# Weighting whole in each step, sums inverted by way of memory, and another opening in a 16-head attention

## What is computed

```python
x = x + layernorm(attention1(layernorm(x)))      # x: 2 x 2048 x 256, float32
x = x + layernorm(ffn_stack(layernorm(x)))       # two layers of windowed attention and gated feed forward

def attention1(x):                               # 16 heads of 16, 2 batches: 32 heads
    q, k, v = rope(x @ Wq.T + bq), rope(x @ Wk.T + bk), x @ Wv.T + bv
    scores = einsum('bhtd,bhsd->bhts', q, k) / 4 # 2048 x 2048 for each of 32 heads
    attn = softmax(scores, axis=-1)
    return einsum('bhts,bhsd->bhtd', attn, v) @ Wo.T + bo
```

## Time and profile before

| | |
|---|---|
| median of 3 runs | 3482.14 us (3476.58 to 3494.06) |
| the profiled execution | 3474.07 us, of which the trace spans 3472.3 us |
| PE, DVE, ACT, POOL busy | 93%, 72%, 65%, 23% of the span |
| projections, until the attention block | 0 to 124 us |
| opening of the attention | 140 to 203 us |
| steps of the attention | 203 to 1866 us |
| end of the attention, output phase | 1866 to 1945 us |
| feed forward and final phase | 1945 to 3472 us |
| DMA | 107.50 MB, mean 31 GB/s |

### The profile page before, as it was taken

The page is one execution under the profiler, slowest core; times in us unless marked ns, Lnnn a source line. Parts: engine busy times, 40 slices in busy tenths (PEclk is TensorE's granted clock), DMA queues, the critical chain, the costliest instruction groups (busy, mean ns, idle before and its releaser), DMA issues. The chain is left out here.

```text
span 3472.3 us, 61794 instructions
## 1 busy us (share of the span) xinstructions
PE 3231.1 (93%) x23464; PEld 2003.4 (58%) x23464; DVE 2487.7 (72%) x4740; ACT 2263.8 (65%) x4950; POOL 804.2 (23%) x992
## 2 busy tenths in 40 slices
PE   8799999999999999999996599999999999999996
PEld 7544333334433343434433478888888888888885
DVE  7458767778867787878862577777777777777775
ACT  5357657567765677757774566666666766676663
POOL 6400000000000000000001643344433444443442
PEclk9659868789977898969988799999999999999998
DMA  5413313133223233223222200000000000000001
GB/s 162 125 19 44 44 23 44 23 44 44 39 27 41 26 44 44 38 28 41 31 29 75 102 1 1 0 0 0 0 0 1 33 1 0 0 0 0 0 1 66
DMA packets 55354, 107.50 MB, mean 31 GB/s; under 512 B 21744, under 2 KB 34032, under 8 KB 48368
## 3 DMA queue, kind: packets, MB, share of 16 engines
q1 hardware_dynamic: 50608, 103.36, 16.8%
q10 hardware_dynamic: 4544, 1.38, 0.2%
HBM read 70.61 MB, written 25.17 MB: 28 GB/s over the span
## 5 line engine op out<-in xcount | busy, mean ns | idle before, releaser
L670 ACT ACTIVATE probs<-scores 128x512 f32<-128x512 f32 x2048 | 1114.9, 596 | 525.3 <-PE scores L607 489.6
L702 DVE TENSOR_REDUCE mx<-aux 128x1 f32<-128x1024 f32 x976 | 1190.6, 1224 | 364.6 <-PE aux L565 360.4
L565 PE MATMUL aux<-k_stack,q_stack 48*128 48x512 f32 x2000 | 943.1, 524 | 36.7 <-DVE mx L702 34.5
L607 PE MATMUL scores<-q_stack,k_stack 50*128 50x512 f32 x2048 | 857.9, 499 | 0.0
L619 PE MATMUL pv<-probs,v_ones 128*32 128x256 f32 x8192 | 745.5, 440 | 0.1
L607 PEld LDWEIGHTS scores<-q_stack,k_stack 50*128 50x128 f32 x2048 | 348.4, 209 | 507.4 <-ACT probs L670 469.1
L565 PEld LDWEIGHTS aux<-k_stack,q_stack 48*128 48x128 f32 x2000 | 396.0, 211 | 174.2 <-DVE mx L702 165.8
L619 PEld LDWEIGHTS pv<-probs,v_ones 128*32 128x32 f32 x8192 | 170.4, 114 | 342.0 <-issue 321.5
L536 POOL CAST m_parts<-head_max 128x16 fp32r<-128x16 f32 x32 | 6.3, 196 | 1516.6 <-DVE head_max L695 1516.6
L1242 PE MATMUL bank<-VO,w_sb 128*128 128x128 f32 x2816 | 328.8, 277 | 1.5 <-ACT VO L1329 1.5
L1242 PEld LDWEIGHTS bank<-VO,w_sb 128*128 128x128 f32 x2816 | 323.2, 194 | 2.5 <-ACT VO L1329 2.5
(11 more groups left out here) (175 smaller groups left out, 4664.0 us busy)
## 6 DMA issues: line engine op xcount, KB each, us to landing
q_stack<-qk_dram SPq DMA_DIRECT2D x192, 128.0 KB, 5.3
k_stack<-qk_dram SPq DMA_DIRECT2D x192, 128.0 KB, 7.5
qk_dram<-qkT_hi SPq DMA_DIRECT2D x32, 256.0 KB, 3.1
qk_dram<-qkT_lo SPq DMA_DIRECT2D x32, 256.0 KB, 3.6
VO<-o_stage SPq DMA_DIRECT2D x128, 32.0 KB, 8.3
totals<-o_stage SPq DMA_DIRECT2D x128, 32.0 KB, 7.9
out<-x_sb SPq DMA_DIRECT2D x9, 384.0 KB, 4.3
wqkv_sb<-in_wqkv SPq DMA_DIRECT2D x2, 1536.0 KB, 7.1
```

The costliest lines, as they stand in the source:

```text
L565: return nc.tensor.matmul(out, q_stack[max_rows, n % BODY, tile * P:(tile + 1) * P], k_stack[max_rows, n % BODY, keys * 512:(keys + 1) * 512],
L607: last = nc.tensor.matmul(out, k_stack[0:SCORE_ROWS, n % BODY, s * P:(s + 1) * P], q_stack[0:SCORE_ROWS, n % BODY, j * 512:(j + 1) * 512], ...
L670: nc.scalar.activation(probs[:, e % PROBS], scores[:, item_of_exp(e) % BANKS1], ACT.Exp, scale=float(D1) ** -0.5).then_inc(act_emptied, 1)
L702: nc.vector.tensor_reduce(mx[:, n % BODY, tile, half:half + 1], aux[:, unit % 2].rearrange("p a k -> p (a k)"), AX.X, ALU.max).then_inc(dv ...
```

## The change

- The weighting of a step is whole: four matmuls of 512 columns, two steps later, between block 1 and block 2. The two maximum tiles before it fill one unit of `aux`, the two after it the other. `pv` is copied one exponential later.
- The sums of a head go as one row for each block to `sums_dram`, come back as 128 partitions x 16, are inverted on DVE in one small instruction a head (`invert_sums`), go back to memory and are read from there 16 times over into `inverse`. For the last 8 heads DVE does half of the multiplications.
- In the opening the differences use rows 0 to 47 of PE and so the loads for scores; each maximum tile is issued between the two matmuls of a difference, and behind the second stands a matmul from row 64 on into `pv`, whose result nobody reads. Head 1 is loaded for scores before the opening, and POOL fills the minus ones buffer by buffer.
- Wo and its bias are loaded during the attention, into a buffer that the feed forward phase later uses for small tiles; these become views of it, with the same instructions.

```diff
         @block.sync
...
                 sp.wait_ge(pv_copied, n + 1)
-                if n % CHUNK == 0 and c > 0:
-                    sp.wait_ge(divided, BLOCKS * c)
                 for j in range(BLOCKS):
-                    for to, row in ((outputs[place:place + D1, c], VW * j), (totals[place:place + D1], VW * j + D1)):
-                        sp.dma_start(to[:, j * 512:(j + 1) * 512], o_stage[row:row + D1, n % 2]).then_inc(outputs_moved, 16)
+                    columns = slice(j * 512, (j + 1) * 512)
+                    sp.dma_start(sums_dram[0, n:n + 1, columns], o_stage[VW * j + D1:VW * j + D1 + 1, n % 2]).then_inc(sums_stored, 16)
+                    sp.dma_start(outputs[place:place + D1, c, columns], o_stage[VW * j:VW * j + D1, n % 2]).then_inc(outputs_moved, 16)
+
+            def load_sums(n):
+
+                sp.wait_ge(sums_stored, 16 * BLOCKS * (n + 1))
+                sp.dma_start(sums[:, n % 2], sums_dram[0, n].rearrange("(p c) -> p c", p=P)).then_inc(sums_loaded, 16)
+
+            def store_inverse(n):
+
+                sp.wait_ge(sums_inverted, n + 1)
+                sp.dma_start(sums_dram[1, n].rearrange("(p c) -> p c", p=P), sums[:, n % 2]).then_inc(inverse_stored, 16)
+
+            def spread_inverse(n):
+
+                sp.wait_ge(inverse_stored, 16 * (n + 1))
+                if n % CHUNK == 0 and n > 0:
+                    sp.wait_ge(divided, BLOCKS * (n // CHUNK))
+                sp.dma_start(inverse[n % CHUNK * D1:(n % CHUNK + 1) * D1], sums_dram[1, n].partition_broadcast(D1)).then_inc(inverse_loaded, 16)
 
             load(0, SECOND, for_max_loaded)
-            load(1, SECOND, for_max_loaded)
-            sp.wait_ge(minus_ones_made, 1)
-            load(0, 0, for_scores_loaded)
+            for n in range(2):
+                sp.wait_ge(minus_ones_made, n + 1)
+                load(n, 0, for_scores_loaded)
+                if n == 0:
+                    load(1, SECOND, for_max_loaded)
             load_rows(0)
+            load_output_weights(sp)
...
+                if n >= 2:
+                    store_inverse(n - 2)
                 if n >= 1:
                     move_outputs(n - 1)
                 if n + 1 < NH:
                     load_rows(n + 1)
+                if n >= 2:
+                    spread_inverse(n - 2)
+                if n >= 1:
+                    load_sums(n - 1)
+            store_inverse(NH - 2)
             move_outputs(NH - 1)
+            spread_inverse(NH - 2)
+            load_sums(NH - 1)
+            store_inverse(NH - 1)
+            spread_inverse(NH - 1)
...
         @block.gpsimd
...
-                pool.wait_ge(for_max_loaded[n], 16 * LOADS)
+                rows = slice(0, SPLIT_ROWS)
+                pool.wait_ge(for_scores_loaded[n], 16 * LOADS)
...
-                if n % CHUNK == 1 and n > 1:
-                    divide(n // CHUNK - 1)
+                if n % CHUNK == 2 and n > 2:
+                    for j in range(BLOCKS):
+                        divide(n // CHUNK - 1, j)
+                    pool.wait_ge(divided, BLOCKS * (n // CHUNK))
...
         @block.tensor
...
+            def weigh(step):
+
+                n, s = divmod(step, TB)
+                if s == 0:
                     pe.wait_ge(v_made, n + 1)
                     if n:
                         pe.wait_ge(pv_copied, n)
-                pe.wait_ge(act_emptied, item_of_exp(BLOCKS * (TB * n + s + 1) - 1) + 1)
-                columns = slice(half * HALF, (half + 1) * HALF)
+                pe.wait_ge(act_emptied, item_of_exp(BLOCKS * (step + 1) - 1) + 1)
                 for j in range(BLOCKS):
...
+                    last = nc.tensor.matmul(pv[VW * j:VW * (j + 1)], v_ones[:, n % BODY, s, :], probs[:, (BLOCKS * step + j) % PROBS],
+                                            start=(s == 0), stop=(s == TB - 1), skip_group_check=True, tile_position=(0, VW * j))
+                last.then_inc(pv_done, 1)
+
+            def first_difference(t, k):
...
+                out, rows = for_act(2 * t + k), slice(0, SPLIT_ROWS)
+                nc.tensor.matmul(out, q_stack[rows, n, tile * P:(tile + 1) * P], k_stack[rows, n, (2 + k) * 512:(3 + k) * 512], start=True, stop=False)
+                for_dve(t, k)
+                nc.tensor.matmul(out, q_minus_first[rows, t], k_stack[rows, n, k * 512:(k + 1) * 512], start=False, stop=True).then_inc(act_filled, 1)
+                nc.tensor.matmul(pv[:], q_stack[max_rows, n, tile * P:(tile + 1) * P], k_stack[max_rows, n, k * 512:(k + 1) * 512], start=True, stop=True)
...
                     if rows_here(p, i):
                         maximum_rows(p // 2 + 1)
-                    if j == 0:
-                        weigh_earlier(step, 2, 1)
-                    if j == (3 if step % TB == 1 else 2):
-                        weigh_earlier(step, 1, 0)
...
+                    if j == 1 and step >= 2:
+                        weigh(step - 2)
+            weigh(NH * TB - 2)
+            weigh(NH * TB - 1)
 
         @block.scalar
...
-                    if i == BLOCKS + 1 and p % 2 == 0 and p > 0:
+                    if i == BLOCKS + 2 and p % 2 == 0 and p > 0:
                         copy_outputs(p // 2 - 1)
...
         @block.vector
...
-            def invert_totals(c, j):
-
-                dve.wait_ge(outputs_moved, 16 * 2 * BLOCKS * CHUNK * (c + 1))
-                here = totals[:, j * 512:(j + 1) * 512]
-                nc.vector.reciprocal(here, here).then_inc(inverted, 1)
+            def invert_sums(n):
+
+                dve.wait_ge(sums_loaded, 16 * (n + 1))
+                nc.vector.reciprocal(sums[:, n % 2], sums[:, n % 2]).then_inc(sums_inverted, 1)
...
-                    if p % 2 == 1 and i % SPAN == SPAN - 1 and n % CHUNK == 0 and n > 0:
-                        invert_totals(n // CHUNK - 1, i // SPAN)
-            for j in range(BLOCKS):
-                invert_totals(NH // CHUNK - 1, j)
...
+                    if p % 2 == 0 and i == 3 and n >= 2:
+                        invert_sums(n - 2)
+            invert_sums(NH - 2)
+            invert_sums(NH - 1)
+            for j in range(BLOCKS // 2, BLOCKS):
+                divide(NH // CHUNK - 1, j)
```

More of the change, by code:

```diff
@@ L365 @@
 VW = 32
-HALF = 256
 SPAN = TB // 2
@@ L566, in score_for_max @@
                                         start=True, stop=True)
-            def difference(t, k, out):
-                n, tile = divmod(t, TB)
-                piece = [i for i, (head, start, stop) in enumerate(Q_MINUS_PIECES) if head == n and start <= tile < stop][0]
-                pe.wait_ge(q_minus_made, piece + 1)
-                minus = q_minus_first[max_rows, t]
-                pe.wait_ge(for_max_loaded[n % BODY], 16 * LOADS * (n // BODY + 1))
-                nc.tensor.matmul(out, q_stack[max_rows, n % BODY, tile * P:(tile + 1) * P], k_stack[max_rows, n % BODY, (2 + k) * 512:(3 + k) * 512], start=True, stop=False)
-                nc.tensor.matmul(out, minus, k_stack[max_rows, n % BODY, k * 512:(k + 1) * 512], start=False, stop=True).then_inc(act_filled, 1)
             def for_act(item):
@@ L615, in weigh @@
                         pe.wait_ge(pv_copied, n)
-                pe.wait_ge(act_emptied, item_of_exp(BLOCKS * (TB * n + s + 1) - 1) + 1)
-                columns = slice(half * HALF, (half + 1) * HALF)
+                pe.wait_ge(act_emptied, item_of_exp(BLOCKS * (step + 1) - 1) + 1)
                 for j in range(BLOCKS):
-                    last = nc.tensor.matmul(pv[VW * j:VW * (j + 1), columns], v_ones[:, n % BODY, s, :], probs[:, (BLOCKS * (TB * n + s) + j) % PROBS, columns],
-                                            start=(s == 0 and half == 0), stop=(s == TB - 1 and half == 1), skip_group_check=True, tile_position=(0, VW * j))
-                if half == 1:
-                    last.then_inc(pv_done, 1)
-            def weigh_earlier(step, back, half):
-                if step >= back and step - back < NH * TB:
-                    weigh((step - back) // TB, (step - back) % TB, half)
+                    last = nc.tensor.matmul(pv[VW * j:VW * (j + 1)], v_ones[:, n % BODY, s, :], probs[:, (BLOCKS * step + j) % PROBS],
+                                            start=(s == 0), stop=(s == TB - 1), skip_group_check=True, tile_position=(0, VW * j))
+                last.then_inc(pv_done, 1)
+            def first_difference(t, k):
+                n, tile = divmod(t, TB)
+                piece = [i for i, (head, start, stop) in enumerate(Q_MINUS_PIECES) if head == n and start <= tile < stop][0]
+                pe.wait_ge(q_minus_made, piece + 1)
+                pe.wait_ge(for_scores_loaded[n], 16 * LOADS)
+                out, rows = for_act(2 * t + k), slice(0, SPLIT_ROWS)
[3 more added lines that the diff above has]
+                nc.tensor.matmul(pv[:], q_stack[max_rows, n, tile * P:(tile + 1) * P], k_stack[max_rows, n, k * 512:(k + 1) * 512], start=True, stop=True)
             for t in range(OPENING):
@@ L632, in _ @@
                 for k in range(2):
```

(8 more changed lines are left out.)

83 lines of the change are left out of this document (43 added, 40 removed).

## The result

| | before | after |
|---|---|---|
| median | 3484.73 us of 4 runs (3476.58 to 3494.06) | 3163.7 us of 4 runs (3163.28 to 3165.74) |
| profiled execution | 3474.07 us | 3163.34 us, span 3161.5 |
| granted clock, mean | see the earlier trace rows | 0.971 |
| first scores of the steps | 203.1 us | 203.7 us |
| copy behind the last weighting starts | 1867.4 us | 1572.9 us |

The ratio is 0.9079, 95% interval 0.9055 to 0.9103: 321 us or 9.2% faster. The forecast was 3140 us, with a range of 3045 to 3275.

What follows compares the result with a forecast made beforehand. PE's order, with its clock, was taken as the bound. Steps ending at 1536 instead of 1866 (330 us less) and 9 us at the end gave 3474 - 330 - 9 = 3135, stated as 3140 us; range 3045 to 3275.

Steps and rivals of the forecast that it cites:

- The visit: PE going to the weighting and back: 0.39 us that streams nothing at full clock, 0.45 at half; whole visit 1.00 us.
- The rival that gave the fixed cost to the weighting: Only the page's drain goes; the rest of the fixed cost stays with the weighting: 2.80 us a step, 3221 us; chance 9%.
- The clock: PE's clock over the steps: 10% of their time at half clock instead of 28%, mean step 2.63 us.
- The three falls at the inversions: DVE's long inversions, twelve inside the loop, make PE wait up to 2.6 us and its clock fall; these go.
- The step: Attention step at full clock: period 2.40 us, 2.46 with the score banks, 2.54 with what a head adds.
- The last 24 steps: End of the attention steps, without maximum tiles: left at 2.40 us, since banks and ACT's four exponentials bind.
- The opening: Before the steps: DVE starts at 160.5 us instead of 148.01, four passes a tile, over at 194 instead of 203.
- The end: From the copy behind the last weighting to PE's output product: 16.7 us against 21.3, gain 9 us (4 to 11).
- The inversion and late sums: 32 small inversions of some 0.2 us; DVE waiting on late sums was given nothing, as a rival 1%.
- the unchanged clock: Rival: steps stay at half clock 28% of the time, 2.81 us a step, sum 3225 us; chance 22%.
- the starved engines: Rival: the whole weighting starves ACT and DVE, 2.80 us a step, 2.88 with the clock, 3270 us; chance 6%.
- the half clock for most of the time: Slower rival: PE falls to half clock for most of the steps; at 80% a step is 3.52, 3610 us; chance 4%.

## Why the prediction was right, and where two errors met

The predicted mechanism of the visit held, and 3140 against 3163.7 is inside the range. But two terms of the steps were wrong in opposite senses, 71 us too few and 44 too many, so that the forecast came this close is in part luck.

- **The visit: right.** 0.39 us fixed at full clock and 0.45 at half gave 1.00 and 1.86 us for a whole weighting; measured 1.00, and 1.86 at half clock early in the steps (210.80 to 212.66). The rival that gave the fixed cost to the weighting falls, and the run with 256 columns in one visit shows it. The estimate from the Trainium skill (TensorEngine Tiling (Array Packing), Key Properties, with the drain of TensorE: Matmul & The Clock Gate), 53 ns each way, is not what these traces have: a visit costs 0.39 us beyond what it streams. The whole weighting alone brought over 225 us, and with it the share of half clock between 215 and 1500 us went from 28% to 8%, so much of this gain is the clock.
- **The clock: wrong, too careful, and its reason was wrong.** I took 10% of the time at half clock, since "the wait at the transpose stays". It stayed, at 0.49 us (I had 0.6), and brought no fall. This alone made the forecast 44 us too long: 488 steps of 2.54 are 1240 us, not 1284. The three falls at the inversions were read rightly: in the kernel with the whole weighting alone they are the only ones behind the start of the steps. But I came down from 28% because "the known causes of more than half of it are removed", the inversions and the old opening. With both removed and the weighting in halves 22% are left (clock 0.89). What raised the clock is the whole weighting, for which the argument on the clock has nothing.
- **The step: wrong, too short.** 2.54 was predicted, 2.67 is the mean; without head ends 2.46 and 2.61. The step that failed is the one that added 0.13 us for the score banks to a period made from DVE's, and halved it. The pieces were there: tile at 1.72, its exponential 2.3 to 2.9, against 1.72 and 2.25 to 2.85 in the trace. What was missing was to follow them once round, to the same tile one step later. With the prediction's own distances this gives 0.33 + 1.00 + 0.58 + 0.60 + 0.05 = 2.56 us, with those of the trace after 2.62 (0.43 from the waiting tile to the weighting), and leaves DVE with time to spare. A delay in one loop is not halved into the period of another: the longer loop sets it. Halved reductions and the moved weighting both show which loop it is.
- **The last 24 steps** should take 2.40 without maximum tiles. They take 2.61, as the same loop is in them (from one weighting to the next 2.60 us at 1537.80 and 1540.39):

```profile
1537.80 1.07 PE L644 MATMUL pv<-probs,v_ones 128*32 128x512 f32 x8
1538.79 0.96 PE L632 MATMUL scores<-q_stack,k_stack 50*128 50x512 f32 x3
1539.97 0.49 PE L632 MATMUL scores<-q_stack,k_stack 50*128 50x512 f32 x1 [0.22 <-ACT probs L696]
1540.39 1.06 PE L644 MATMUL pv<-probs,v_ones 128*32 128x512 f32 x8
```

  Together the steps take 1368 us where 1342 were predicted: 71 too few for their length (their first 10 us, still at half clock, among it), 44 too many for the clock.
- **The opening: start right, rest wrong.** DVE starts at 159.78, predicted 160.5:

```profile
144.65 5.69 POOL L557 TENSOR_SCALAR q_minus_first<-q_stack 48x512 fp32r<-48x512 f32 x2 [9.27 <-DMA k_stack<-qk_dram]
156.75 2.76 POOL L557 TENSOR_SCALAR q_minus_first<-q_stack 48x1024 fp32r<-48x1024 f32 x1 [6.40 <-DMA k_stack<-qk_dram]
...
159.78 1.23 DVE L737 CUSTOM_DVE_ANT_0 excess<-aux,excess 128x1024 f32<-128x1024 f32 x1 [37.97 <-POOL mx L560]
```

  But I let paired rows raise the clock part of the way ("I take 194"). It is 0.50 until 214 us, a tile takes 1.87 us with waits of DVE for ACT in between, and the steps begin at 203.7. Price of this step: 9.7 us. Its later start and its shorter tiles cancel, which is why the old opening does as well.
- **The end: right.** 15.8 us, predicted 16.7. The small round trips by way of memory are the cost, not the inversion:

```profile
1572.87 0.59 ACT L704 COPY o_stage<-pv 128x512 f32<-128x512 f32 x1 [1.19 <-PE pv L644]
...
1580.52 0.25 DVE L750 RECIPROCAL sums<-sums 128x16 f32<-128x16 f32 x1 [38.18 <-DMA sums<-sums_dram]
...
1588.71 1.19 PE L850 MATMUL psY<-wo_bo_sb,ident 128*128 128x256 f32 x2 [15.91 <-PEq L402]
```

- **The inversion and late sums: right.** 0.24 us an instruction, and DVE doesn't wait for sums in the loop.
- **The sum.** 3135 predicted for the profiled execution, + 26 for the steps, + 9.7 for the opening, - 1.7 for the end (10.7 against 9), - 5.6 in the rest: 3163.4, measured 3163.34.

Of the rivals, the unchanged clock, the starved engines and the half clock for most of the time didn't come. The first is nearly what the kernel with halves did: there the clock fell at head ends with the inversions gone. The whole weighting took these falls away; it shortened the wait too, but that this is the cause isn't shown.

## What to carry to other kernels

If PE visits another kind of matmul in the middle of a stream, price the visit from two distances (into it, out of it) and not from the columns, and make one visit of two where buffers allow it. Then follow each buffer loop once round to the same instruction one period later, and take the longest; don't average loops or add a part of one to another. A wait of under a microsecond can cost more than its length through the clock, as 0.45 us more of it brought falls of 1.2 us each here: look which waits stand ahead of a fall, and move the waiting instruction behind work that is ready, as the transpose here, for 15 us.

## What the runs showed of the hardware

- Going to the weighting (eight instructions for 32-column parts of PE, float32) and back costs 0.39 us at 2.4 GHz and 0.45 at 1.2, by the earlier trace rows. A visit takes the same 1.00 us at full clock with 8 instructions of 512 columns as with 16 of 256.
- The clock fell behind waits of PE of 0.94 and 1.75 us at head ends (and of 0.65 in the kernels with halves), among steps in which PE was otherwise busy, and did not behind 0.49 us. The shortest such falls lasted 3.4 us. The Trainium skill (TensorE: Matmul & The Clock Gate, HAM oscillation) describes such falls for kernels in which TensorE works in bursts and waits for DMA longer than it computes; these rows show them behind single waits in a stream that is dense for the rest.
- The same wait can do nothing nine times and then be followed by a fall each time (0.94 us, before and after 620 us). No row shows what differs.
- In the opening the clock stayed at 0.50 from 161 us on through a stream of matmuls in which the waits are short, and rose at 214 us, ten after the steps had begun; without the unread matmul it rose at 219.
- When it rises goes with the weighting and not with the opening: at 245 us in both kernels with halves (before, and the one with the new opening), at 219 and 221 in the two with whole weighting behind the old opening, at 255 with the weighting one tile earlier. Here the kernel with halves and the new opening, then the old opening with whole weighting:

```profile
220.00:240.00 20.00, 20.00 (x114) 6.49 (x116) 11.58 (x10) 10.32 (x20) 0.00 (x0) 0.50 0.00 1
220.00:230.00 10.00, 9.54 (x60) 3.70 (x56) 8.07 (x8) 7.15 (x14) 0.00 (x0) 0.97 0.01 1
```

  By what the clock tells the two orders apart, no run shows.
